# Re-ordering the four engines' programs inside one pipelined iteration of a two-layer attention kernel

## The reference

```
# layer 0: 8 heads of 32, over 512 positions; q serves as query, key and value
q      = x^T Wq^T
logits = (scale q q^T * mask_k + (1 - mask_k) * -1e30) * mask_q
x      = x + ((softmax(logits) q) Wo^T)^T
# layer 1: 16 heads of 32, over the 256 rows of x, model width 512
xn     = rms_norm(x, g_norm) * (1 + s) + t        # s, t from cond @ W_emb + b_emb
q,k,v  = split(xn W_qkv);  q = rms_norm(q, g_q);  k = rms_norm(k, g_k)
o      = softmax(q k^T * 32^-0.5) v
x      = x + o + o W_out
```

## Time and profile before

| | us |
|---|---|
| median of 3 runs | 1366.49 (1365.67 to 1368.57) |
| the profiled execution | 1369.83 |
| its span, first to last instruction | 1367.8 |
| PE busy | 1265.5 (93%) |
| DVE busy | 1079.0 (79%) |
| POOL busy | 787.5 (58%) |
| ACT busy | 770.8 (56%) |

### The profile page before, as it was taken

One profiled execution on the slowest core, in us unless ns is written; L12 is line 12 of the kernel. 1 busy time (PEld: TensorE's weight loads), 2 busy tenths in 40 slices (PEclk: granted clock), 3 DMA queues, 4 the chain that ended last, 5 costly groups with the idle time before them and its releaser, 6 DMA issues.

```text
span 1367.8 us, 20709 instructions
## 1 busy us (share of the span) xinstructions
PE 1265.5 (93%) x6896; PEld 592.0 (43%) x6896; DVE 1079.0 (79%) x932; ACT 770.8 (56%) x1377; POOL 787.5 (58%) x391
## 2 busy tenths in 40 slices
PE   2877899999999999999999999999999999999976
PEld 1523344444444444444444444444444444443432
DVE  5355798888888898888888798888889798888543
ACT  1243657565657666565656656565766656565522
POOL 0232747675674757675674757576574757556622
PEclk8588899999999999999999999999999999999988
DMA  7304251625435261625435261635435172534040
GB/s 247 100 11 126 57 142 38 172 77 130 118 89 145 59 165 40 170 79 128 120 86 146 48 172 47 162 87 122 127 77 147 40 181 52 137 88 109 16 109 15
DMA packets 77702, 142.99 MB, mean 105 GB/s; under 512 B 21280, under 2 KB 22816, under 8 KB 77600
## 3 DMA queue, kind: packets, MB, share of 16 engines
q1 hardware_dynamic: 68880, 126.17, 36.8%
q10 hardware_dynamic: 8720, 15.51, 3.6%
HBM read 32.02 MB, written 8.39 MB: 30 GB/s over the span
## 4 chain that ended last, share of the span: by engine, by line
PE 78%; DVE 11%; ACT 4%; issue 3%; DMA 2%; POOL 1%; ACTq 1%; POOLq 0%; DVEq 0%; SPq 0%
PE PX L440 22%; PE PO L383 9%; PE PS L360 9%; PE PX L467 7%; DVE NM L1043 6%; PE PS L372 5%; PE PO L403 4%; PE PX L307 4%; PE PM L331 4%; DVE NM L1036 3%; PE PM L392 2%; PE PM L458 2%; PE PO L406 2%; PE PX L418 2%; PE PM L340 2%
## 5 line engine op out<-in xcount | busy, mean ns | idle before, releaser
L710 ACT ACTIVATE E<-PS,KBIAS 128x512 f32<-128x512 f32 x512 | 339.1, 687 | 255.1 <-PE PS L360 234.4
L440 PE MATMUL PX<-WQKV,XNT 128*128 128x512 f32 x768 | 399.7, 611 | 15.6 <-ACT XNT L827 12.2
L1036 DVE TENSOR_REDUCE NM<-PM 128x4 f32<-128x2048 f32 x128 | 293.3, 2292 | 100.0 <-PE PM L331 97.0
L1282 POOL TENSOR_TENSOR E<-E 128x1024 f32<-128x1024 f32 x112 | 276.4, 2480 | 162.7 <-PE PO L383 141.0
L1312 POOL TENSOR_TENSOR KQLO<-E 128x1024 f32<-128x1024 f32 x64 | 151.6, 2368 | 253.8 <-ACT E L717 253.8
L360 PE MATMUL PS<-B,A 97*128 97x512 f32 x512 | 282.6, 594 | 9.7 <-ACT E L710 6.3
L1294 POOL TENSOR_TENSOR RQK<-RQK,HALF 128x16 f32<-128x16 f32 x64 | 201.3, 3145 | 38.1 <-DVE RQK L1123 34.8
L717 ACT ACTIVATE E<-PS 128x512 f32<-128x512 f32 x256 | 147.2, 597 | 118.0 <-PE PS L372 108.9
L1043 DVE TENSOR_REDUCE NM<-PM 128x8 f32<-128x2048 f32 x64 | 146.7, 2292 | 40.3 <-PE PM L340 40.0
L440 PEld LDWEIGHTS PX<-WQKV,XNT 128*128 128x128 f32 x768 | 132.8, 192 | 90.9 <-issue 64.3
L360 PEld LDWEIGHTS PS<-B,A 97*128 97x128 f32 x512 | 94.5, 194 | 139.3 <-issue 91.2
(11 more groups left out here) (80 smaller groups left out, 1407.4 us busy)
## 6 DMA issues: line engine op xcount, KB each, us to landing
A<-QHI SPq DMA_DIRECT2D x256, 64.0 KB, 2.0
B<-QHI SPq DMA_DIRECT2D x256, 64.0 KB, 2.0
A<-KQHI SPq DMA_DIRECT2D x128, 128.0 KB, 2.4
B<-KQHI SPq DMA_DIRECT2D x128, 128.0 KB, 2.4
XB<-x SPq DMA_DIRECT2D x16, 512.0 KB, 4.0
A<-QLO SPq DMA_DIRECT2D x128, 64.0 KB, 2.0
B<-QLO SPq DMA_DIRECT2D x128, 64.0 KB, 2.0
X<-x ACTq DMA_DIRECT2D x16, 512.0 KB, 4.8
```

The source lines that it names most:

```text
L440: last = mm(PX[:, :], XNT[:, c, t * P:(t + 1) * P], WQKV[:, c, part * DM:(part + 1) * DM], start=(c == 0), stop=(c == 3))
L710: fn(E[:, probs(seg, i, g), h, :], PS[n % 2][:, :], ACT.Exp, bias=KBIAS[:, g, b:b + 1], scale=SCALE).then_inc(exp_done, 1)
L1036: v.tensor_reduce(NM0[:, q, :].rearrange("p (h k) -> p h k", k=KB0)[:, :, kb], PM[:, :, :], axis=AX.X, op=ALU.max, negate=True).then_inc(m ...
L1282: g_.tensor_tensor(running(seg, i)[:, heads_, :], running(seg, i)[:, heads_, :], E[:, probs(seg, i, g), heads_, :], ALU.add).then_inc(done, 1)
```

## The change

No operation is added, dropped or given to another engine, and no wait condition is rewritten: each still names the operation that it waits for. What changes is the order of the calls in the four lists. The diff, cut to the places that matter (the first part is PE's list):

```diff
+                step_a(0, 0)
                 if l1:
                     qk(i, 0, 0)
-                step_a(0, 0)
                 step_a(0, 1)
                 if l1:
-                    qk(i, 0, 1)
+                    qk(i, 0, 1, 2, 3)
                 step_a(0, 2)
-                    qk(i, 0, 2)
                 step_a(0, 3)
...
                 if l0:
                     weights_summed0("A", i, 0)
-                if l1:
-                    heads_rows(i, i - 1, 0)
+                    values_weighted0("A", i, 0, 3)
...
                 step_b(1, 3)
+                if l1:
+                    heads_rows(i, i - 1, 3)
+                if o1:
+                    out1(i, i - 2, 0, 0, 1, 2)
+                if l1:
+                    maxima1(i, i - 1, 0)
...
+                step_b(3, 3)
                 if l1:
                     maxima1(i, i - 1, 3)
-                step_b(3, 3)
-                if l1:
-                    values1(i, 0, 0, 1)
+                if l0:
+                    values_weighted0("B", i, 1, 2)
+                    values_weighted0("B", i, 1, 3)
+                if l1:
+                    values1(i, 0, 0)
                     rows1(i, i - 1)
-                if l0:
-                    values_weighted0("B", i, 1, 2)
+                    values1(i, 0, 1)
                 if p0:
                     maxima0(i, i + 1, 0, 0)
...
                 step_c(3, 0)
+                if p0:
+                    maxima0(i, i + 1, 0, 3)
                 if l1:
                     values_and_sums1(i, i - 1, 1)
-                if p0:
-                    maxima0(i, i + 1, 0, 3)
                 step_c(3, 1)
+                step_c(3, 2)
+                if p0:
+                    rows0(i, i + 1, 0)
+                step_c(3, 3)
+                if l0:
+                    norm_rows(i, i)
                 if l1:
                     values_and_sums1(i, i - 1, 2)
-                step_c(3, 2)
-                step_c(3, 3)
-                if p0:
-                    rows0(i, i + 1, 0)
-                if l0:
-                    norm_rows(i, i)
```

ACT's list (extract):

```diff
                 step_c(0, 1)
+                if l0:
+                    take_context0("B", i, i, 1)
                 step_c(0, 2)
                 step_c(0, 3)
                 step_c(1, 0)
-                if l0:
-                    take_context0("B", i, i, 1)
                 step_c(1, 1)
+                if l1:
+                    keep_x1(i, i - 1)
                 step_c(1, 2)
                 if l1:
                     values1(i, i - 1, 1)
-                    keep_x1(i, i - 1)
+                if l0:
+                    load_residual(i, i)
+                if p0:
+                    round_query(i, i + 1, 1)
                 step_c(1, 3)
-                if l0:
-                    load_residual(i, i)
```

POOL's list:

```diff
                     add_keys0("A", i, 1, True)
+                    masked_out(i, i)
                     add_keys0("A", i, 2, True)
-                    masked_out(i, i)
...
                 if l0:
+                    scale0(i, i, 0)
+                    add_keys0("B", i, 1, True)
                     add_keys0("B", i, 1, False)
-                    add_keys0("B", i, 1, True)
-                    scale0(i, i, 0)
                     add_keys0("B", i, 2, False)
                     add_keys0("B", i, 2, True)
                     add_keys0("B", i, 3, True)
```

More of the change, by code:

```diff
@@ L573, in iteration @@
                 step_b(1, 1)
-                if l0:
-                    values_weighted0("A", i, 0, 3)
+                if l1:
+                    heads_rows(i, i - 1, 0)
+                step_b(1, 2)
                 if l1:
                     heads_rows(i, i - 1, 1)
-                step_b(1, 2)
                 if p0:
@@ L612, in iteration @@
                     maxima1(i, i - 1, 2)
+                step_b(3, 0)
+                if o1:
+                    out1(i, i - 2, 1, 2)
                 step_b(3, 1)
+                step_b(3, 2)
                 if o1:
-                    out1(i, i - 2, 1, 2, 3)
-                step_b(3, 2)
+                    out1(i, i - 2, 1, 3)
+                step_b(3, 3)
                 if l1:
                     maxima1(i, i - 1, 3)
-                step_b(3, 3)
-                if l1:
-                    values1(i, 0, 0, 1)
-                    rows1(i, i - 1)
                 if l0:
                     values_weighted0("B", i, 1, 2)
+                    values_weighted0("B", i, 1, 3)
+                if l1:
+                    values1(i, 0, 0)
+                    rows1(i, i - 1)
+                    values1(i, 0, 1)
                 if p0:
@@ L633, in iteration @@
                     weights_summed0("B", i, 1)
-                    values_weighted0("B", i, 1, 3)
                 step_c(0, 2)
-                if l1:
-                    values1(i, 1, 0)
+                step_c(0, 3)
                 if p0:
                     maxima0(i, i + 1, 0, 1)
-                step_c(0, 3)
-                if l1:
-                    values1(i, 1, 1)
                 step_c(1, 0)
                 if l1:
-                    values1(i, 1, 2)
+                    values1(i, 1, 0, 1)
                 step_c(1, 1)
@@ L911, in iteration @@
                     round_heads(i, i - 1, 2)
+                    round_heads(i, i - 1, 3)
+                step_b(1, 2)
                 step_b(1, 3)
-                if l1:
-                    round_heads(i, i - 1, 3)
                 if l0:
@@ L974, in iteration @@
                 step_c(3, 3)
+                if l1:
+                    take_context1(i, i - 1, 2)
             def loads():
@@ L1199, in iteration @@
                     split1(i, i - 1, 0)
+                if o1:
+                    context1(i - 1, i - 2, 3)
+                if l1:
                     split1(i, i - 1, 1)
@@ L1229, in iteration @@
                     maxima0(i, i + 1, 0, 2)
-                if l1:
-                    invert1(i, i - 1, 0)
+                    split0(i, i + 1, 1)
                 if l0:
@@ L1242, in iteration @@
                     norm(i, i)
-                if p0:
-                    split0(i, i + 1, 1)
+                if l1:
+                    invert1(i, i - 1, 0)
                 if l0:
```

100 lines of the change are left out of this document (39 added, 61 removed).

## The result

| | before | after |
|---|---|---|
| median, us | 1366.08 (1364.38 to 1368.57, 4 runs) | 1394.37 (1386.81 to 1397.84, 4 runs) |
| the profiled execution | 1369.83 | 1392.77 |
| its span | 1367.8 | 1390.7 |
| PE busy | 1265.5 (93%) | 1258.7 (91%) |

The ratio is 1.0198, 95% interval 1.0152 to 1.0244: 28 us slower. The forecast was slower by 7 us, 1373.5, with a range up to 1383. The time lies outside it, above the stretch that rival 4 named (1379 to 1390) too; the four executions run from 1386.8 to 1397.8.

A forecast was written before the change was run, and what follows sets the result against it. PE's list plus its waits bounds the kernel at 77.07 us an iteration. PE's order gives 76.8, the port 0.8 more (taken as 77.4), the DMA 0.5: 77.9, or +7 us, 1373.5 us; range 1358 to 1383.

The forecast's parts named there:

- rival 4: DMA path sets the period, load_x 1.5 us closer, first scores 1.5 to 2 us late: 1379 to 1390 us; chance 0.18.
- The order on PE: PE's new list: waits and tile switches gone, new waits added; 77.07 falls to 76.8 us an iteration, lower bound 76.4.
- the wait for XNT: PE at `qk` at the start of each iteration: more work ahead of it removes a 1.0 us loss.
- those at `rows1`: PE's wait at `rows1`: value products and one chunk ahead of it remove 0.4 us an iteration.
- tile switches: PE's list: fewer islands of tiled groups (19 to 18) and column-tiled runs (13 to 12) gain 0.3 us an iteration.
- The wait from `out0` to `rows0`: End of PE's list: `rows0` can start 6.0 us after `out0`, with 4.5 us of PE work there.
- The end: End of the iteration: new PE wait of 1.5 us against 0.0 before; net 1.3 us more an iteration.
- The copy of context B before score (1, 0): Segment C, ACT: score (1, 0) waits for the exponential behind the copy, 0.25 us, bounds 0 and 0.5.
- The port: Segment B: POOL's add first by 0.4 us, holding off DVE's add; cost 0.8 us an iteration, bounds 0 and 1.3.
- These terms together: PE's order plus the POOL and DVE lock: sum 77.6, from the lower bound 77.2, taken as 77.4 us an iteration.
- The DMA of the maxima: `load_x` 1.0 us closer to the small DMA of `rows0` delays first scores: 0.5 us an iteration, bounds 0 and 1.5.
- Rival 1: Removed waits decide, DVE's delay absent or swallowed, DMA in time: 76.4 to 76.8 an iteration, 1354 to 1359 us; chance 0.25.

The follow-up runs named there:

- a_pool: Changed kernel with GpSimd's segment B order as before (two adds of key block 1, then scale0); ratio 1.0107 to the kernel before.
- b_pool: Kernel before with GpSimd's new segment B order (scale0 ahead of the adds of block 1, those two exchanged); ratio 1.0030 to the kernel before.
- hyb_load: Changed kernel with segment C, iteration end and GpSimd's segment B order as before, load_x after 18 of 24 stack0 DMAs; ratio 0.9996 to the kernel before.
- a_split: Changed kernel with split0(i+1, 1) on DVE back behind norm, nothing else; ratio 1.0121 to the kernel before.
- b_split: Kernel before with split0(i+1, 1) on DVE moved directly behind the third maxima0; ratio 1.0079 to the kernel before.
- a_load: Changed kernel with load_x issued after 18 of the 24 DMAs of stack0(i+1, 0) instead of all; ratio 1.0078 to the kernel before.
- a_pool_load: Changed kernel with GpSimd's segment B order as before and load_x after 18 of 24 stack0 DMAs; ratio 1.0000 to the kernel before.
- b_load: Kernel before with load_x issued after 18 of the 24 DMAs of stack0(i+1, 0), nothing else; ratio 0.9986 to the kernel before.

## Why the prediction was right in direction and wrong in size

*The order on PE.* Confirmed: the wait for XNT went (12.2 us), so did those at `rows1` (3.8 to 1.2). The 0.3 us of tile switches was not tested apart; PE's busy time fell by 7 us, where it gives 4 to 5. The wait from `out0` to `rows0` came as worked out, 5.9 us against 6.0. The end costs what was forecast, 1.4 us for 1.5, but as two waits, by start times 0.9 ahead of the maxima and 0.5 at `rows0`.

*The copy of context B before score (1, 0).* Forecast 0.25, and wrong in its place: the score does not wait, the second `maxima0` ahead of it does, 0.4 us in start times, for the bank that DVE takes the sums from. The prediction had the semaphore of the maxima and not those of the banks.

*The port.* Confirmed in mechanism and size for segment B: POOL first by 0.38 us (0.4 forecast), 3.04 us in place of 1.21, a wait of 0.8 us at line 392 in the mean (0.45 to 1.15 idle; 0.95 forecast), 12 us of the total in a_pool. b_pool shows that POOL's order alone costs 4 us, a third of it; the rest needs PE's new list beside it. That the same port would be met in segment A (hyb_load) the prediction does not have.

These terms together were forecast at 77.4 us. Measured: interval less start of the first score is 74.5 at full clock, and with a first score at 2.9 that makes 77.4. The mean of 79.4 is this, 1.7 for the first score (4.6 against 2.9) and 0.3 for the two stretches at 1.2 GHz, a term that the prediction put at nothing.

*The DMA of the maxima: the step that failed.* The prediction took 0.5 us for it, "bounds 0 and 1.5", from `load_x` coming 1.0 us closer. `load_x` came only 0.4 closer (2.0 ahead of `norm_rows` instead of 2.4). But the first score is late by 1.7 us in the mean, where it was 0.4 before: over three times the term, and above its upper bound. What it left out is `split0(i + 1, 1)`. The change moves it from behind the last reduction to ahead of it, 7 us earlier, and I noted the move and priced only its 0.7 us on DVE. On SP's queue 24 DMAs are behind it. They now follow `load_x` at once, the first one or two stand ahead of the small one, and it lands 6.5 us behind XB instead of 5.4. a_split takes that back (0.8% of the time), b_split shows it in the kernel before (+0.8%), a_load removes nearly the whole wait (1.2%). Of the 1.7 us, 0.4 were there before, 0.6 are left with the late `split0` and the nearer `load_x` (a_split), near the 0.5 that was priced, and 0.7 are the step that was left out. Rival 4 came nearest in its time and its place, first scores 1.5 to 2 us late, but its mechanism, `load_x` 1.5 us closer, was not this one.

*The baseline.* Rival 1 held that up to 0.9 us an iteration could be won. With the two large costs repaired the time is only that of before (a_pool_load): the end of the iteration keeps its 1.4 us, and the middle `rows0` waits for a DVE that POOL holds off. With the old end (hyb_load) 0.6 us are won behind the middle `rows0`, and most of it is lost ahead of it in the same manner. Whether an order exists that keeps the gain is not shown.

With what the Trainium skill says of the port pair (SBUF — State Buffer, SBUF: two separate sides) the runs agree in both kernels: the later of the two add instructions ends about a full duration behind the earlier one's end (1.08 us of 1.21 for DVE). What the Trainium skill says of turns between queues (DMA: Bandwidth & Descriptors, Queues, rings and completion order) is not the whole account here: a small DMA beside a full queue of another engine took up to 5.3 us to land after, against 1.8 at best.

## What to carry to other kernels

When an operation moves, price what its semaphore lets go on other queues, before its own duration: 0.7 us of DVE, moved over 7 us earlier, cost 11 us in the kernel before (b_split), because it let one to four of 24 DMAs out ahead of one small one. Issue large loads early enough ahead of a small DMA on the critical path: with `load_x` 4.5 us ahead of `norm_rows` instead of 2.0, the first score is on time in most iterations, with six stack DMAs right in front of the small one. And two engines that share a port can differ by 0.1 us in who comes first and by 1 to 2 us in what it costs: read the order of arrival, not the durations. When a repair shortens the period, look for what now meets that did not meet before: the middle `rows0` does not wait in the change, and waits in every repair of it that brings the first score early.

## What was not expected of the hardware

- With XB issued 2.4 us ahead of `norm_rows`, one to four 64 KB stack DMAs issued ahead of the small one (8 KB, another engine's queue) move its landing from 5.4 to 6.5 us behind the issue of XB (b_split). With XB issued 4.9 us ahead and six stack DMAs between (b_load), it lands 2.2 us behind its own issue, against 2.8 before. SP issues such DMAs every 0.6 us.
- A blocked DVE add does not show as a late start: its record begins right behind the reduction ahead of it and is 3.04 to 3.34 us long, with no idle time before it. In a view of busy time the wait is counted as work: DVE's adds took 123.3 us after against 98.7 before for the same 80 instructions. An operation of 0.17 us became one of 2.19 in the same way (hyb_load).
- A late first score costs more than its wait where the clock falls behind it: 3.4 us at 1.2 GHz, and an interval 1.6 us longer, in two of the 12 intervals after.
